# Two cross-attentions and one linear attention of a four-layer decoder unrolled into pipelines, and the attention strips' score banks taken three in turn

## The reference

```python
def _L1_xattn_ref(query, key_, value, Wq_w, Wq_b, Wk_w, Wk_b, Wv_w, Wv_b):     # one head of 128
    Q, K, V = query @ Wq_w.T + Wq_b, key_ @ Wk_w.T + Wk_b, value @ Wv_w.T + Wv_b
    attn = softmax(Q @ K.T / sqrt(128), axis=-1)
    return attn @ V
def _L2_xattn_ref(c, q, w_cq, b_cq, w_c, b_c, w_q, b_q, W_l, b_l):             # c is x, q the context
    cq = jnp.einsum('bcd,bqd,d->bcq', c, q, w_cq) + b_cq
    s = (c @ w_c + b_c)[:, :, None] + (q @ w_q + b_q)[:, None, :] + cq
    a = jax.nn.softmax(s, axis=2)
    c2q_att = jnp.einsum('bcq,bqd->bcd', a, q)
    b_att = jax.nn.softmax(jnp.max(s, axis=2), axis=1)
    q2c_att = jnp.einsum('bc,bcd->bd', b_att, c)[:, None, :]
    x = jnp.concatenate([c, c2q_att, c * c2q_att, c * q2c_att], axis=-1)
    return x @ W_l.T + b_l
def _L3_attn_ref(x, Wq, bq, Wk, bk, Wv, bv, Wp, bp):                           # 16 heads of 8
    q, k, v = x @ Wq + bq, x @ Wk + bk, x @ Wv + bv
    q, k = elu(q) + 1, elu(k) + 1
    return (q @ (k.T @ v)) @ Wp + bp                                           # per head
```

## Time and profile before

| | us |
|---|---|
| three runs | 2878.23, 2880.04, 2885.68 (median 2880.04) |
| profiled execution | 2875.15, of which the span is 2873.4 |
| PE busy | 2471.7 (86% of the span) |
| DVE busy | 1607.7 (56%) |
| ACT busy | 1220.6 (42%) |
| POOL busy | 1027.8 (36%) |

### The profile page before, as it was taken

How to read it: one execution, slowest core, us unless ns; L and a number is a source line. 1 busy time by engine, 2 the same in 40 slices (tenths; PEclk the granted TensorE clock), 3 DMA queues, 4 the chain that set the end, 5 groups by cost and what they waited for, 6 DMA issues and landing times. The chain is left out here.

```text
span 2873.4 us, 46663 instructions
## 1 busy us (share of the span) xinstructions
PE 2471.7 (86%) x16071; PEld 1461.3 (51%) x16123; DVE 1607.7 (56%) x3705; ACT 1220.6 (42%) x3200; POOL 1027.8 (36%) x891
## 2 busy tenths in 40 slices
PE   5979997698768999999999989997787997797998
PEld 2446665354435555555555555555445444454343
DVE  3544544463467777777777777774453223462333
ACT  1324451253036666666666666663340110253121
POOL 2010002011067777877777777772100001000000
PEclk7989998797779999999999999999796895898899
DMA  2100000100010000000000000000100000100010
GB/s 60 23 19 1 1 1 2 14 3 1 0 49 5 20 14 12 16 16 24 9 10 23 9 13 20 16 1 1 16 1 15 22 22 0 23 2 23 22 33 18
DMA packets 42278, 41.71 MB, mean 15 GB/s; under 512 B 6913, under 2 KB 31150, under 8 KB 42045
## 3 DMA queue, kind: packets, MB, share of 16 engines
q1 hardware_dynamic: 42044, 38.69, 5.1%
HBM read 33.10 MB, written 0.52 MB: 12 GB/s over the span
## 5 line engine op out<-in xcount | busy, mean ns | idle before, releaser
L2924 POOL TENSOR_TENSOR l1fb_p<-l1fb_p,l1fb_rden 128x640 f32<-128x640 f32 x192 | 240.4, 1252 | 259.0 <-DVE l1fb_rden L2991 259.0
L2916 POOL TENSOR_TENSOR l1fb_rinv<-l1fb_ssq,neghalf 128x8 f32<-128x8 f32 x192 | 315.1, 1641 | 8.5 <-DVE l1fb_ssq L2981 8.4
L3120 PE MATMUL ps<-l1fb_wqkv,l1fb_xs 128*128 128x512 f32 x576 | 298.3, 628 | 9.2 <-DVE l1fb_xs L2947 4.3
L3076 ACT ACTIVATE l1fb_p<-ps,l1fb_shift 128x128 f32<-128x128 f32 (+1 forms) x768 | 282.1, 392 | 0.3
L2986 DVE TENSOR_REDUCE l1fb_shift<-ps 128x4 f32<-128x640 f32 x192 | 157.8, 822 | 108.0 <-PE ps L3150 106.5
L2918 POOL TENSOR_TENSOR l1fb_qk<-l1fb_qk,l1fb_rinv 128x512 f32<-128x512 f32 x192 | 202.2, 1053 | 15.0
L3057 ACT ACTIVATE l1fb_sq<-ps 128x512 f32<-128x512 f32 x192 | 114.8, 598 | 176.0 <-PE ps L3120 164.5
L3076 ACT ACTIVATION_READ_ACCUMULATOR l1fb_p<-ps,l1fb_shift 128x1 f32 x768 | 168.7, 220 | 0.0
L3136 PE MATMUL ps<-ident,l1fb_qk 128*128 128x128 f32 x768 | 126.4, 287 | 36.6 <-DVE l1fb_attT L3000 28.7
L3150 PE MATMUL ps<-l1fb_kT,l1fb_qT 64*128 64x128 f32 (+1 forms) x1536 | 147.6, 311 | 0.0
L2974 DVE TENSOR_TENSOR l1fb_r<-ps,l1fb_turn_tab 128x256 f32<-128x256 f32 x384 | 143.0, 414 | 0.0
(11 more groups left out here) (714 smaller groups left out, 5484.6 us busy)
## 6 DMA issues: line engine op xcount, KB each, us to landing
l1fb_wqkv<-in_L_ffn_Wqkv SPq DMA_DIRECT2D x24, 256.0 KB, 2.7
l3f_w<-in_L_ffn_W SPq DMA_DIRECT2D x21, 256.0 KB, 3.1
l2f_w<-in_L_ffn_W SPq DMA_DIRECT2D x16, 256.0 KB, 3.0
l1fb_wqkv<-in_L_ffn_Wqkv SPq DMA_DIRECT2D x6, 512.0 KB, 3.8
l1fb_wo<-in_L_ffn_Wo SPq DMA_DIRECT2D x6, 512.0 KB, 4.3
l1fb_w<-in_L_ffn_W SPq DMA_DIRECT2D x6, 341.0 KB, 2.9
l3x_k<-l3x_k SPq DMA_DIRECT2D x8, 128.0 KB
l1fb_w<-in_L_ffn_W SPq DMA_DIRECT2D x6, 128.0 KB
```

The source lines that it names most:

```text
L2916: nc.gpsimd.tensor_tensor(w.rinv[:, u, :], w.ssq[:, u, :], chip.neghalf[:, 0:8], ALU.pow).then_inc(*w.unit_norm.end(f"rinv{u}"))
L2924: nc.gpsimd.tensor_tensor(p, p, w.rden[:, c, :, :].rearrange("p j q -> p (j q)").unsqueeze(2).to_broadcast([P, 2 * QT, SEEN]), ALU.mult)\
L3076: last = nc.scalar.activation(w.p[:, c % 4, j, q, 0:hi - lo], ps[:, SCORE_BANK(c) + j, lo:hi], ACT.Exp, bias=w.shift[:, c, j, q:q + 1], ac ...
L3120: nc.tensor.matmul(ps[:, PROJ_BANK(u), :], w.xs[:, x.odd, q * P:(q + 1) * P], w.wqkv[:, col:col + 512], start=True, stop=True)\
```

## The change

- **Strips.** `Strips.bank()` gives each strip's scores bank (2 x unit + i) mod 3: scores take banks 0 to 2 and transposed scores banks 3 to 5, in turn. Waits are per bank, for the maximum or the exponential of three banks before. DVE reduces each bank by itself (128 x 512 twice), and each bank's scores are counted.
- **`l1_xattn`.** No loop: all four batches are written out in a pipeline. PE reads `x_tok` and `ctxT` where they lie. The value bias is added to the residual by POOL (`rest`), which is exact because the softmax weights sum to one; the division by the sum and the addition of `rest` are one DVE instruction. ACT copies keys and values of batches 0 and 1, the values of 2 and 3, and half of the turned weights. Keys and values of batches 2 and 3 stand between scores.
- **`l2_xattn`.** The same form. `b_l` is added by POOL. The second branch is new: the negated maximum is spread by a one-row matmul (`to_all`), ACT takes the exponential of `top` in its column, `sums` gives the sum and the weighted sum of the tokens, and DVE folds the mean into the weights, `tilt` = fourth weight x mean + first weight. An output tile is three products.
- **`l3_attn`.** Two pairs in one pipeline, 512 columns per operation where possible. Biases of keys and queries are one-row matmuls of 512 columns, one each per pair; those of values and output are added by DVE and POOL. ACT copies the second pair's tokens and both `oT`.
- **Loads.** `L1_xattn_Wv_b`, `L2_xattn_b_l`, `L3_attn_bv`, `L3_attn_bp` go from `ROWS` to `SPREAD`; the number of transfers stays.

```diff
+    def bank(self, b, g, u, i):
+        return (2 * self.pair(b, g, u) + i) % 3
@@ strips_pe
-    def scores_free(t, u):
+    def scores_free(t, u, i):
         b, g = h.group(t)
-        n = h.pair(b, g, u)
+        n = 2 * h.pair(b, g, u) + i
...
-        if n >= 2:
-            eng.wait_ge(*h.maxed.of(n - 2))
+        if n >= 3:
+            eng.wait_ge(*h.maxed.of(n - 3))
     def scoresT_free(t, u, i):
...
-        if n >= 2:
-            eng.wait_ge(*h.exped.of(n - 2))
+        if n >= 3:
+            eng.wait_ge(*h.exped.of(n - 3))
...
             elif slot < LAG:
-                scores_free(slot, u)
                 for i in range(2):
-                    nc.tensor.matmul(ps[:, 2 * (h.pair(*h.group(slot), u) % 2) + i, :], chip.ident_b[:, :],
+                    scores_free(slot, u, i)
+                    nc.tensor.matmul(ps[:, h.bank(*h.group(slot), u, i), :], chip.ident_b[:, :],
                                      chip.ident_b[:, :].unsqueeze(1).to_broadcast([P, 4, P]), start=True, stop=True)
@@ strips_dve
-        nc.vector.tensor_reduce(dst, src, AX.X, ALU.max, negate=True).then_inc(*h.maxed.one())
+        for i in range(2):
+            bank = h.bank(b, g, u, i)
+            eng.wait_ge(*h.scored.of(2 * h.pair(b, g, u) + i))
...
+            nc.vector.tensor_reduce(dst, src, AX.X, ALU.max, negate=True).then_inc(*h.maxed.one())
@@ l1_xattn, tensor
-            with eng.Fori(0, B // PAIR) as b:
...
-                        nc.tensor.matmul(out, cT[i][:, kt * P:(kt + 1) * P], w["L1_xattn_Wv_w"][:, 0, :], start=True, stop=False)
-                        last = nc.tensor.matmul(out, chip.ones[0:1, 0:P], w["L1_xattn_Wv_b"], start=False, stop=True)
...
+            keys(0)
+            values(0)
+            tokens(0)
+            tokens(1)
+            queries(0)
+            queries(1)
+            keys(1)
+            values(1)
+            scores(0)
+            keys(2)
+            values(2)
+            scores(1)
+            keys(3)
+            values(3)
+            turned(0)
+            turned(1)
+            scores(2)
+            outputs(0)
+            scores(3)
+            outputs(1)
+            turned(2)
+            turned(3)
+            outputs(2)
+            outputs(3)
@@ l2_xattn, tensor
+            tokens(0)
+            tokens(1)
+            scores(0)
+            scores(1)
+            row(0)
+            turned(0)
+            to_all(0)
+            row(1)
+            turned(1)
+            to_all(1)
+            sums(0)
+            scores(2)
+            attended(0)
+            sums(1)
+            scores(3)
+            attended(1)
+            joined(0)
+            row(2)
+            turned(2)
+            to_all(2)
+            joined(1)
+            row(3)
+            turned(3)
+            to_all(3)
+            sums(2)
+            attended(2)
+            sums(3)
+            joined(2)
+            attended(3)
+            joined(3)
@@ l3_attn, tensor
+            def inputs(i):
+                nc.tensor.matmul(tiled(keys), chip.ones[0:1, 0:P], w["L3_attn_bk"].unsqueeze(1).to_broadcast([1, TILES, D]), start=True, stop=False)
+                nc.tensor.matmul(queries, w["L3_attn_bq"], fp(chip.ones)[0:1, 0:N], start=True, stop=False)
+                eng.wait_ge(*(dve if i == 0 else act).done(f"xT{i}"))
...
+            tokens(0)
+            tokens(1)
+            inputs(0)
+            inputs(1)
+            products(0)
+            attended(0)
+            products(1)
+            projected(0)
+            attended(1)
+            projected(1)
```

More of the change, by code:

```diff
@@ L1619, in _, with keys @@
         @block.scalar
         def _(eng):
[L1621 to L1627 removed]
+            def keys(b):
+                eng.wait_ge(*pe.done(f"k{b}"))
+                nc.scalar.activation(kT[:, b, :], ps[:, KBANK[b], :], ACT.Identity, bias=w["L1_xattn_Wk_b"]).then_inc(*act.end(f"k{b}"))
@@ new lines, in tokens, with queries @@
+            def tokens(i):
+                for x in range(PAIR * QT):
+                    last = nc.tensor.transpose(ps[:, 6 + i, x * P:(x + 1) * P], chip.x_tok[:, PAIR * i + x // QT, x % QT, :], chip.ident[:, :])
+                last.then_inc(*pe.end(f"xT{i}"))
+            def queries(i):
+                eng.wait_ge(*(dve.done("xT0") if i == 0 else act.done("xT1")))
+                nc.tensor.matmul(ps[:, 4 + i, :], w["L1_xattn_Wq_w"][:, 0, :], xT[:, 2 * i:2 * i + 2, :].rearrange("p b s -> p (b s)"),
+                                 start=True, stop=True).then_inc(*pe.end(f"q{i}"))
@@ new lines, in scores @@
+            def scores(b):
+                eng.wait_ge(*dve.done(f"q{b // 2}"))
+                if b < 2:
+                    eng.wait_ge(*act.done(f"v{b}"))
+                else:
+                    eng.wait_ge(*dve.done(f"k{b}"))
+                    eng.wait_ge(*act.done(f"c{b - 2}"))
+                    eng.wait_ge(*dve.done(f"c{b - 2}"))
+                for qt in range(QT):
+                    last = nc.tensor.matmul(ps[:, pair(b) + qt, :], qT[:, b, qt * P:(qt + 1) * P], kT[:, b, :], start=True, stop=True)
+                last.then_inc(*pe.end(f"s{b}"))
@@ new lines, in column, with turned @@
+            def column(b):
+                eng.wait_ge(*dve.done(f"shift{b}"))
+                nc.scalar.activation(col[:, b, :], top[:, b, :], ACT.Exp, bias=shift[:, b:b + 1]).then_inc(*act.end(f"col{b}"))
+            def turned(b):
+                eng.wait_ge(*pe.done(f"t{b}"))
+                if b >= 2:
+                    eng.wait_ge(*pe.done(f"att{b - 2}"))
+                nc.scalar.activation(prT[:, b % 2, 0, :, :].rearrange("p t q -> p (t q)"), ps[:, pair(b), :], ACT.Copy).then_inc(*act.end(f"c{b}"))
@@ new lines, in row, with turned @@
+            def row(b):
+                eng.wait_ge(*dve.done(f"top{b}"))
+                for qt in range(QT):
+                    last = nc.tensor.transpose(small(b)[0:1, qt * P:(qt + 1) * P], top[:, b, qt:qt + 1], chip.ident[:, :])
+                last.then_inc(*pe.end(f"row{b}"))
+            def turned(b):
+                eng.wait_ge(*dve.done(f"norm{b}"))
+                for qt in range(QT):
+                    for kt in range(CT):
+                        last = nc.tensor.transpose(ps[:, pair(b) + qt, kt * P:(kt + 1) * P], pr[:, b % 2, qt, kt * P:(kt + 1) * P], chip.ident[:, :])
+                last.then_inc(*pe.end(f"t{b}"))
@@ new lines, in joined @@
+            def joined(b):
+                eng.wait_ge(*act.done(f"att{b}"))
+                eng.wait_ge(*dve.done(f"tilt{b}"))
+                eng.wait_ge(*dve.done(f"xatt{b}"))
+                if b:
+                    eng.wait_ge(*dve.done(f"sum{b - 1}"))
+                for qt in range(QT):
+                    at = slice(qt * P, (qt + 1) * P)
+                    for k, (part, weight) in enumerate(((xT[:, b, at], tilt[:, b % 2, :]), (att[:, b % 2, at], w["L2_xattn_W_l"][:, 1, :]),
+                                                        (xatt[:, b % 2, at], w["L2_xattn_W_l"][:, 2, :]))):
+                        last = nc.tensor.matmul(z[:, qt, :], part, weight, start=k == 0, stop=k == 2)
+                last.then_inc(*pe.end(f"z{b}"))
```

821 lines of the change are left out of this document (505 added, 316 removed).

## The result

The changed kernel takes 2772.07 us (median of 4 runs, 2771.23 to 2774.31) against 2879.14 for the kernel before, timed beside it: ratio 0.9632, 95% interval 0.9613 to 0.9652. Forecast was 2792, range 2765 to 2830. The profiled execution has a span of 2770.1, 103.3 less than before.

| | l0a | l1a | l1x | l2a | l2x | l3a | l3x | the five others |
|---|---|---|---|---|---|---|---|---|
| before | 152.6 | 232.2 | 68.8 | 117.9 | 81.2 | 61.0 | 199.8 | 1924.1 |
| after | 152.4 | 223.4 | 35.9 | 110.7 | 56.0 | 30.3 | 200.3 | 1925.5 |
| forecast of the difference | +1.5 | -3 | -27 | -3 | -25 | -27 | -4.5 | 0 |
| difference | -0.2 | -8.8 | -32.9 | -7.2 | -25.2 | -30.7 | +0.5 | +1.4 |

The account below looks back on a forecast made before the run. PE's standing still and low clock in `l1x`, `l2x` and `l3a` were taken as the bound. 2875.15 less 27, 25, 27 and 9 (strips) gave 2787 profiled; with 4.9 for the median 2792, range 2765 to 2830.

Parts of the forecast that it names:

- The chain: `l1x`: PE's work in order, slow start 7.5, fast part 26.7, waits 1.2, end 4.8; sum 40.2, taken as 42.
- the 5 added for DVE's order: `l2x`: raised from 51 to 56 because DVE's list is long and strictly ordered.
- the 8 of waits: `l3a`: 8 us for the way from first keys over minimum, exponential and sum to the products.
- The value between the clock's levels: `l3a`: 34 us, taken between 29 at the fast level and 38 at the slow level throughout.
- The guess that single-row matmuls: `l1x`'s first 20 us: single-row matmuls and small products go with the clock at 0.50; new stages have wide ones.
- rival A: New stages: the clock stays down, `l1x` 66, `l2x` 71, `l3a` 38, gains together 45, total 2835; chance 0.17.
- Per unit without side work 0.18: Strips' steady part: the wait for the exponential goes, saving 0.18 us a unit, bounds 0.05 and 0.33.
- The +3 for POOL: `l1a`'s steady strips: 3 us lost to a stall on POOL that then comes first.
- The circle: Strips' prologue: filler, scores, maximum and hand-overs make 2.25 a unit, 0.65 more; +6.5 in `l3x`.
- rival D: Strips: more and shorter PE pauses bring its clock down; if all units fall, 2913; chance 0.02.
- Rival B: Strips: all idle time goes and transfers hide the prologue's circle; strips -25, total 2776; chance 0.13.

Follow-up runs that it names:

- e5: Kernel before without the one-row bias matmuls of `l1x`, `l2x` and `l3a`, loops kept: 2853.6 us.
- e6: Changed kernel with one-row bias matmuls back behind products of 128 columns, 16 in `l1x` and 24 in `l3a`: 2822.5 us.
- e9: Changed kernel without the four one-row bias matmuls of 512 columns in `l3a`: 2761.6 us.
- e10: Changed kernel with four score banks in the prologue, `l2x`'s weight scaling earlier in DVE's list, and `l3a`'s four wide biases over 128 rows: 2754.84 us.
- e8: Changed kernel with bias matmuls of 128 columns back, 16 in `l1x` and 24 in `l3a`, each over 128 rows: 2786.8 us.
- e1: Kernel before with the change of the strips alone, the three looped stages kept: 2873.9 us, ratio 0.9976.
- e2: Changed kernel with two banks for transposed scores as before, scores keeping three: 2813.6 us.
- e3: Changed kernel with four score banks in the strips' prologue instead of three: 2758.02 us.

## Why the prediction was right, step by step

**`l1x`, forecast 42, measured 35.9.** The chain was right. Up to the second queries, at 721.34, it took 6.65 for 7.5, since the clock rose 6.0 us into the stage. The fast part of 26.7 with waits of 1.2 took 24.9, of which 0.17 was waiting: rows beside one-row matmuls had priced the products too high (0.97 for 0.85). The end took 4.4 for 4.8, and the 2 added for ACT's copies were not needed. The gain of 32.9 is against a lucky `l1x` of before; against 75.2 it is 39.

**`l2x`, forecast 56, measured 56.0, in part by luck.** Waits inside were 8.5 (four for scaled weights, 7.4, and one of 1.1), for 10 allowed; but PE's work, 33 at the fast level, was 44.44 busy, because nearly half of the stage ran at 0.50 (mean 0.77), where I had a slow start only, at 3.5 us. These 8 us too many were met by the 5 added for DVE's order and by 3 too many in the end (3.0 for 4.8) and the waits. No run shows what brought the clock down there.

**`l3a`, forecast 34, measured 30.3.** The terms were 16.5, 8 and 4.8; the mis-sized one is the 8 of waits, which were 2.8 (0.58, 1.54 and 0.69). The value between the clock's levels was right by its mean of 0.78. My list of what was removed gave the gap between turns, the tails and the biases together; e5 and e6 show that nearly all of it was the biases (27, and 3 for the rest), and e9 and e10 that the four wide ones I kept cost 7.3 more, 5.7 of it because they have one row.

**The clock.** The guess that single-row matmuls, not a lack of work, held it down was right, and it carried the forecast against rival A. What it called "and small products" was wrong: e8 has as many small ones. I then gave it up for the experiments' theory, and the runs brought it back. What neither had is that one-row matmuls are also longer at the same level.

**Strips, steady part.** Per unit without side work 0.18: measured 3.93 less 3.58 for two, 0.175. Over the stages -11.0 in `l3x`, -7.9 in `l1a`, -5.9 in `l2a`, for 11, 6 and 4. In `l1a` I let 33 units gain, but four in turn take 7.77 for 8.45, 0.17 for each of them. The +3 for POOL did not come: one unit of `l1a` took 1.6 longer, part of it at the slow level (in e1, with the same strips, 0.6), the others did not. e2 shows the mechanism.

**Strips, prologue.** The circle was right (2.23 for 2.25), and so was its own price: 6.9 in `l3x` by e6 and e10, for 6.5. What was missing is the clock: the first values come 12.8 later, and the rest of that is the piece at 0.50, which came with the circle (it is absent in e3) but not in every run that has it (e1, e6). That is near to rival D's mechanism in the prologue, where I had not looked for it; in the steady part it did not show. Rival B fell for this reason too: its -25 would have needed the prologue of e3. The strips gave 15.7 for 9: their steady parts 24.8 for 18, above all `l1a` (7.9 for 3), and their prologues 11 for 9. In `l1a`, `l2a` and `l0a` the circle cost next to nothing (first values at 64.7, 47.5 and 59.5 us of the stage, before 65.7, 48.8 and 58.9), where I had put 0, 1 and 1.5. So 12.8 in `l3x` for 6.5 was in part made up elsewhere: the total of the prologues is right by luck.

Together the pipelines gave 10 more than forecast and the strips 7.
